# A vision block on one NeuronCore: nine token tiles of 128 in place of twelve of 96

## The reference, cut to what matters

```python
h = patches @ W.T + b                                  # 768 -> 192
# first block (input: layernorm of h)
x = _ln(x, ln1_w, ln1_b)
k, v, sr = h @ Wk_a.T, h @ Wv_a.T, sigmoid(h @ Wr_a.T)
y = bi_wkv(decay / Tn, first / Tn, k, v)               # scan over the 36 tokens, both ways, per channel
x = x + sr * y @ Wo_a.T
h = _ln(x, ln2_w, ln2_b)
x = x + sigmoid(h @ Wr_f.T) * (square(relu(h @ Wk_f.T)) @ Wv_f.T)
# second block (input: layernorm of h)
qkv -> softmax attention, 12 heads of 16, within each image -> proj
top-2 of 8 experts per token, each 192 -> 768 -> 192 with gelu
```

## Time and profile before

| | us |
|---|---|
| median of 3 runs (lowest, highest) | 360.93 (359.34, 362.2) |
| the profiled execution | 360.52 |
| its span, first to last instruction | 358.7 |
| PE busy / DVE busy / ACT busy in the span | 328.8 / 209.2 / 188.9 |

### The profile page before, as it was taken

One profiled execution on the slowest core, in us unless ns is written; L12 is line 12 of the kernel. 1 busy time (PEld: TensorE's weight loads), 2 busy tenths in 40 slices (PEclk: granted clock), 3 DMA queues, 4 the chain that ended last, 5 costly groups with the idle time before them and its releaser, 6 DMA issues.

```text
span 358.7 us, 7680 instructions
## 1 busy us (share of the span) xinstructions
PE 328.8 (92%) x2651; PEld 284.8 (79%) x2651; DVE 209.2 (58%) x580; ACT 188.9 (53%) x505; POOL 84.3 (24%) x85
## 2 busy tenths in 40 slices
...
GB/s 268 354 232 0 3 0 1 0 2 0 0 2 0 153 319 122 261 47 48 243 118 108 60 80 92 68 55 76 49 38 43 53 54 54 38 43 55 63 31 25
...
## 3 DMA queue, kind: packets, MB, share of 16 engines
...
## 4 chain that ended last, share of the span: by engine, by line
PE 44%; DVE 15%; DMA 12%; ACT 12%; issue 11%; POOL 2%; DVEq 1%; POOLq 1%; ACTq 0%
DMA out<-ffn 11%; PE banks L1318 7%; PE banks L1348 7%; PE banks L1319 6%; PE banks L1564 3%; PE banks L1415 3%; PE banks L1547 2%; PE banks L1389 2%; PE banks L1459 2%; PE banks L1390 2%; PE banks L1471 2%; ACT patch L842 1%; POOL rs L635 1%; DVE st L974 1%; ACT xh L718 1%
## 5 line engine op out<-in xcount | busy, mean ns | idle before, releaser
L635 POOL TENSOR_TENSOR rs<-va,consts 96x6 f32<-96x6 f32 (+1 forms) x16 | 17.4, 1087 | 199.5 <-DVE va L980 101.3
L1564 PE MATMUL banks<-arena,ffn 128*128 x240 | 42.9, 329 | 0.0
L667 POOL DMA_INDIRECT out<-ffn x20 | 32.3, 1617 | 44.1 <-DVE ffn L1275 37.4
L1564 PEld LDWEIGHTS banks<-arena,ffn 128*128 128x128 f32 x240 | 38.5, 190 | 0.6 <-issue 0.2
L906 ACT ACTIVATE ffn<-banks,chans 128x128 f32<-128x128 f32 x21 | 9.6, 458 | 52.9 <-PE banks L1537 52.9
L657 POOL DMA_INDIRECT vs<-xh_scratch,ffn x21 | 21.9, 1041 | 17.6 <-DVE ffn L1242 9.3
L1415 PE MATMUL banks<-rvw,ffn 128*96 128x192 f32 x144 | 25.4, 327 | 0.5 <-ACT ffn L814 0.5
L1348 PE MATMUL banks<-arena,patch 128*96 128x192 f32 x144 | 25.0, 327 | 0.0
L1348 PEld LDWEIGHTS banks<-arena,patch 128*96 128x96 f32 x144 | 23.1, 163 | 1.7 <-issue 1.2
L1415 PEld LDWEIGHTS banks<-rvw,ffn 128*96 128x96 f32 x144 | 23.3, 163 | 0.8 <-ACT ffn L814 0.8
L738 ACT ACTIVATE ht<-banks,chans 128x288 f32<-128x288 f32 (+1 forms) x24 | 12.6, 583 | 19.3 <-PE banks L1363 19.2
...
## 6 DMA issues: line engine op xcount, KB each, us to landing
...
```

What stands on the lines that cost most here:

```text
L635: pool.tensor_tensor(dst, src, const_("power", T)[:, 0:n * GTILES], ALU.pow).then_inc(rstd_ready, 1)
L667: pool.indirect_dma_start(out[:, :], bass.IndirectOffsetOnAxis(ap=IS[:, j:j + 1], axis=0), YG[j % 2], None, compute_op=ALU.add).then_inc(s ...
L1564: ins = mm(ps[:, 0:C], HST[j % 2][:, 128 * k:128 * (k + 1)], W2[:, bass.ds(e, 1), C * k:C * (k + 1)], start=(k == 0), stop=(k == HB - 1))
```

## The change

Tokens now lie in nine tiles of `T = 128`. Token stages and layer norms work on *batches* of whole tiles, two or three tiles each, listed per kind of layer norm in `BATCH`: tiles 0-2, 3-4, 5-6, 7-8 for the first norm and 0-1, 2-3, 4-5, 6-8 for the other three. The channel stages `kvr` and `qk`, the scans and the attention keep groups of eight images (288 tokens), so their borders no longer fall on those of the batches: `kvr` and `qk` wait for every batch that holds a part of their group, and the reload of values (`vl`) for every stored batch that it needs. `kf` works on batches, 256 or 384 columns. In `wo` the scan's output is laid out by groups and its result by tiles, so `cuts` splits the matmuls of a tile where a group ends. `HT` now holds all 1152 tokens for all four norms in place of `HT` and `HTB` with two groups each, and the waits of `ht_readers` are gone. `OT` holds all tokens too. `ORDER` is written anew; ScalarE takes patches from tile 5 on in place of tile 6; `kvrw` is loaded after the fourth patch tile in place of the fifth. The expert stage is the same.

```diff
-T = 96
-GTILES = GT // T
+T = 128
...
+SPLIT = (0, 2, 4, 6, TILES)
+BATCH = {"a": (0, 3, 5, 7, TILES), "2": SPLIT, "b": SPLIT, "g": SPLIT}
+BT = 3
+
+
+def tiles_of(kind, g):
+
+    return range(BATCH[kind][g], BATCH[kind][g + 1])
+
+
+def slice_of(kind, g):
+    return slice(BATCH[kind][g], BATCH[kind][g + 1])
+
+
+def batch_of(kind, t):
+    return next(g for g in range(G) if t in tiles_of(kind, g))
+
+
+def batches(kind, lo, hi):
+
+    return range(batch_of(kind, lo // T), batch_of(kind, (hi - 1) // T) + 1)
+
+
+def cuts(t, n):
+
+    marks = sorted({T * t, T * t + T} | {x for x in range(0, TOK, n) if T * t < x < T * t + T})
+    out = []
+    for lo, hi in zip(marks, marks[1:]):
+        a, b = lo - T * t, hi - T * t
+        if a == 32 and b > 64:
+            out += [(lo // n, 32, 64), (lo // n, 64, b)]
+        else:
+            out.append((lo // n, a, b))
+    return out
...
 ORDER = """
-tok:0 tok:1 tok:2 stats:a:0 apply:a:0 tok:3 tok:4 tok:5 turn:a:0 kvr:0:0 kvr:1:0 stats:a:1 apply:a:1 turn:a:1 kvr:0:1
-wkv:0:0 kvr:1:1 tok:6 sub:0:0 sub:0:1 sub:0:2 wexp:0:0 wexp:0:1 wkv:0:1 wkv:0:2 wkv:0:3 wexp:0:2 sub:0:3 wexp:0:3
-wexp:0:4 tok:7 wkv:0:4 wkv:0:5 tok:8 tok:9 tok:10 tok:11 kvr:2:0 stats:a:2 stats:a:3 apply:a:2 kvr:2:1 apply:a:3
-turn:a:2 turn:a:3 wexp:0:5 wkv:0:6 rc:0 wkv:0:7 kvr:0:2 kvr:0:3 wkv:1:0 kvr:1:2 kvr:2:2 wo:0 wo:1 kvr:1:3 wkv:1:1
-sub:1:0 sub:1:1 wexp:1:0 wexp:1:1 sub:1:2 sub:1:3 hx:0 hx:1 stats:2:0 apply:2:0 wexp:1:2 wexp:1:3 wkv:1:2 wexp:1:4
-wkv:1:3 wkv:1:4 wkv:1:5 kvr:2:3 turn:2:0 kf:0:0 kf:1:0 stats:2:1 apply:2:1 wexp:1:5 wkv:1:6 rv:0 rv:1 turn:2:1 rc:1
-wkv:1:7 rv:2 kf:0:1 kf:1:1 ff:0 stats:b:0 apply:b:0 wo:2 hx:2 wo:3 hx:3 turn:b:0 stats:2:2 stats:2:3 apply:2:2
-apply:2:3 rv:3 rv:4 qk:0 spread:0:0 rv:5 ff:1 stats:b:1 spread:1:0 turn:2:2 turn:2:3 sc:0:0 vt:0 s:0 exp:0 kf:0:2
-kf:1:2 s:1 s:2 exp:1 s:3 sc:1:0 s:4 s:5 vl:0:0 vl:1:0 vm:0:0 exp:2 exp:3 exp:4 exp:5 apply:b:1 vm:1:0 rv:6 rv:7 rv:8
-ff:2 pt:0 pt:1 turn:b:1 pv:0 pv:1 pt:2 pt:3 stats:b:2 apply:b:2 ot:0 ot:1 pv:2 pv:3 kf:0:3 ot:2 ot:3 qk:1 spread:1:1
-vt:1 vl:0:1 vl:1:1 spread:0:1 turn:b:2 proj:0 base:0 stats:g:0 kf:1:3 apply:g:0 sc:0:1 sc:1:1 s:6 s:7 s:8 s:9 vm:0:1
-vm:1:1 exp:6 exp:7 s:10 s:11 rv:9 exp:8 exp:9 exp:10 exp:11 rv:10 rv:11 ff:3 pt:4 pt:5 turn:g:0 pv:4 pv:5 qk:2
-spread:1:2 logits:0 spread:0:2 vt:2 pt:6 pt:7 stats:b:3 apply:b:3 ot:4 ot:5 pv:6 pv:7 sc:0:2 s:12 s:13 ot:6 ot:7
-turn:b:3 vl:0:2 vl:1:2 exp:12 s:14 s:15 exp:13 exp:14 vm:0:2 proj:1 stats:g:1 apply:g:1 sc:1:2 s:16 qk:3 spread:0:3
-spread:1:3 exp:15 vt:3 exp:16 s:17 exp:17 sc:0:3 s:18 s:19 s:20 s:21 turn:g:1 pt:8 pt:9 pv:8 pt:10 exp:18 exp:19
-exp:20 vm:1:2 logits:1 pv:9 pt:11 sc:1:3 s:22 vl:0:3 exp:21 s:23 ot:8 ot:9 pv:10 pv:11 vl:1:3 exp:22 exp:23 pt:12
-ot:10 ot:11 pt:13 base:1 proj:2 vm:0:3 pv:12 pv:13 vm:1:3 pt:14 pt:15 ot:12 ot:13 pv:14 pv:15 stats:g:2 apply:g:2
-ot:14 ot:15 proj:3 stats:g:3 turn:g:2 logits:2 apply:g:3 turn:g:3 base:2 base:3 logits:3
+tok:0 tok:1 tok:2 stats:a:0 apply:a:0 tok:3 tok:4 tok:5 turn:a:0 kvr:0:0 stats:a:1 apply:a:1 turn:a:1 kvr:0:1 wkv:0:0
+wkv:0:1 kvr:1:0 wkv:0:2 kvr:1:1 sub:0:0 wexp:0:0 sub:0:1 sub:0:2 wexp:0:1 sub:0:3 wexp:0:2 wexp:0:3 wexp:0:4 wkv:0:3
+kvr:2:1 tok:6 wkv:0:4 wkv:0:5 tok:7 tok:8 kvr:2:0 wexp:0:5 stats:a:2 stats:a:3 apply:a:2 apply:a:3 turn:a:2 turn:a:3
+wkv:0:6 rc:0 wkv:0:7 kvr:0:2 kvr:0:3 wkv:1:0 wkv:1:1 kvr:2:2 wo:0 hx:0 wo:1 kvr:1:3 hx:1 sub:1:0 sub:1:1 wexp:1:0
+wexp:1:1 wkv:1:2 stats:2:0 kvr:1:2 sub:1:2 wkv:1:3 wexp:1:2 sub:1:3 wexp:1:3 wexp:1:4 apply:2:0 turn:2:0 kvr:2:3
+wexp:1:5 wkv:1:4 wkv:1:5 stats:2:1 kf:0:0 apply:2:1 kf:1:0 wkv:1:6 rc:1 wkv:1:7 rv:0 rv:1 turn:2:1 wo:2 hx:2 ff:0 wo:3
+hx:3 stats:2:2 stats:2:3 apply:2:2 apply:2:3 kf:0:1 kf:1:1 turn:2:2 turn:2:3 stats:b:0 apply:b:0 turn:b:0 rv:2 rv:3
+ff:1 kf:0:2 kf:1:2 vt:0 stats:b:1 apply:b:1 turn:b:1 rv:4 qk:0 rv:5 spread:0:0 spread:1:0 kf:0:3 kf:1:3 ff:2 stats:b:2
+apply:b:2 turn:b:2 vl:0:0 vm:0:0 sc:0:0 sc:1:0 s:0 s:1 exp:0 exp:1 s:2 exp:2 s:3 s:4 s:5 exp:3 exp:4 rv:6 rv:7 exp:5
+rv:8 ff:3 vt:1 pt:0 pt:1 vl:1:0 stats:b:3 qk:1 spread:1:1 spread:0:1 vt:2 apply:b:3 turn:b:3 pv:0 pv:1 pt:2 pt:3 ot:0
+sc:0:1 s:6 sc:1:1 s:7 s:8 s:9 s:10 exp:6 exp:7 vm:1:0 qk:2 spread:1:2 s:11 spread:0:2 ot:1 pv:2 pv:3 vl:0:1 vl:1:1
+exp:8 exp:9 exp:10 exp:11 vt:3 ot:2 sc:0:2 s:12 vm:0:1 vm:1:1 s:13 s:14 exp:12 exp:13 sc:1:2 s:15 s:16 s:17 pt:4 pt:5
+qk:3 spread:0:3 ot:3 spread:1:3 pv:4 pv:5 pt:6 proj:0 stats:g:0 pt:7 ot:4 pv:6 ot:5 pv:7 vl:0:2 vl:1:2 apply:g:0
+sc:0:3 s:18 exp:14 exp:15 exp:16 exp:17 s:19 s:20 s:21 vm:0:2 pt:8 pt:9 ot:6 ot:7 pv:8 exp:18 exp:19 exp:20 pv:9
+proj:1 vm:1:2 exp:21 turn:g:0 sc:1:3 s:22 pt:10 stats:g:1 s:23 exp:22 vl:0:3 pt:11 ot:8 ot:9 exp:23 pv:10 pv:11 vl:1:3
+logits:0 vm:0:3 ot:10 pt:12 apply:g:1 pt:13 base:0 proj:2 stats:g:2 ot:11 turn:g:1 vm:1:3 pv:12 pv:13 pt:14 pt:15
+ot:12 ot:13 apply:g:2 pv:14 pv:15 turn:g:2 ot:14 ot:15 proj:3 stats:g:3 logits:1 logits:2 apply:g:3 base:1 base:2
+base:3 turn:g:3 logits:3
...
-TOK_BY_ACT = range(6, TILES)
+TOK_BY_ACT = range(5, TILES)
...
-        HTB = KVRW[:, :, :].rearrange("p b n -> p (b n)").rearrange("p (r b t) -> p r b t", r=2, b=2)
+        OT0 = KVRW[:, :, :].rearrange("p b n -> p (b n)")
...
-        XH = sb("xh", [T, 2 * GTILES, C])
-        HT = sb("ht", [128, 2, 2, GT])
+        XH = sb("xh", [T, 2 * BT, C])
+        HT = sb("ht", [128, 2, TOK])
...
-        OT = sb("ot", [128, 2, 2, GT])
+        OT1 = sb("ot1", [128, TOK])
+        OT = (OT0, OT1)
...
-        NACT = 10
+        NACT = 8
...
-                if t == 4:
+                if t == 3:
...
+                    lo = GT * g + GT // 2 * half
+                    for part in batches("b", lo, lo + GT // 2):
...
-                    for job in ht_readers(STEPS, step):
-                        full(act, job)
...
-                                turned_(pe, "a", g)
+                                for part in batches("a", GT * g, GT * (g + 1)):
+                                    turned_(pe, "a", part)
...
-                    c, half = divmod(g, 2)
-                    pe.wait_ge(z_ready, c + 1)
-                    for i, t in enumerate(group_tiles(g)):
+                    for t in tiles_of("2", g):
                         ps = begin(("wo", t))
-                        z0 = Z[c][:, GT * half + T * i:GT * half + T * (i + 1)]
-                        z1 = Z[c][:, CI * NT + T * i:CI * NT + T * (i + 1)]
-                        end(over_channels(ps[0:T, 0:C], (WOW[:, 0, :], WOWODD if half else WOW[:, 1, :]), (z0, z1)), ("wo", t))
+                        pe.wait_ge(z_ready, (T * t + T - 1) // (2 * GT) + 1)
+                        for c, lo, hi in cuts(t, 2 * GT):
+                            at = T * t - 2 * GT * c
+                            mm(ps[lo:hi, 0:C], Z[c][:, at + lo:at + hi], WOW[:, 0, :], start=True, stop=False)
+                        for n, lo, hi in cuts(t, GT):
+                            at = CI * NT + T * t - GT * n
+                            ins = mm(ps[lo:hi, 0:C], Z[n // 2][:, at + lo:at + hi], WOWODD if n % 2 else WOW[:, 1, :], start=False, stop=True)
+                        end(ins, ("wo", t))
                 elif kind == "kf":
                     need("kfw", "rfw", "vfw")
...
-                            turned_(pe, "b", g)
-                        end(over_channels(ps[:, 0:GT], h_(g, 0, GT, HTB), w_(QKVW, 128 * w, 128 * (w + 1))), (n, g))
+                            for part in batches("b", GT * g, GT * (g + 1)):
```

More of the change, by code:

```diff
@@ L147, in jobs_of @@
     kind, x = step[0], step[-1]
-    tiles = range(GTILES * x, GTILES * (x + 1))
     if kind in ("tok", "rv"):
@@ L157, in jobs_of @@
     if kind == "wo":
-        return [("wo", t) for t in tiles]
+        return [("wo", t) for t in tiles_of("2", x)]
     if kind == "kf":
@@ L163, in jobs_of @@
     if kind == "vt":
-        return [("vt", t) for t in tiles]
+        return [("vt", t) for t in tiles_of("b", x)]
     if kind == "sc":
@@ L169, in jobs_of @@
     if kind == "proj":
-        return [("proj", t) for t in tiles]
+        return [("proj", t) for t in tiles_of("g", x)]
     if kind == "logits":
```

192 lines of the change are left out of this document (93 added, 99 removed).

## The result

The changed kernel takes 348.67 us (median of 4 runs, 347.99 to 350.51), the kernel before beside it 361.07: a ratio of 0.9669 (95% interval 0.9615 to 0.9722). The prediction, 351 us in 343.5 to 358.5, held. A later comparison of the same two gave 0.9711 (0.9657 to 0.9766), 349.92 to 362.07. The profiled execution took 347.99 us, its span 345.8. PE is busy 310.9 us in place of 328.8, DVE 196.3 in place of 209.2.

What follows compares the result with a forecast made beforehand. DVE was taken to lead from 28.1 to 115.1 us, then PE to the last `proj`. Terms -1.5 -5.0 -3.2 +1.7 -1.4 = -9.4 on 360.5 us gave 351 us; range 343.5 to 356, or to 358.5 without two rivals.

Steps and rivals of the forecast that it cites:

- To the first scan, -1.5: Start to the first scan (28.1 us before): fewer tiles needed for `kvr:0:1` and `kvr:1:0` moved behind it, -1.5 us.
- First half of the scan, -5.0: To the second scan's start: three `tok` tiles instead of six, shorter norms and fewer DVE waits, -5.0 us (-3 to -6).
- Second half, -3.2: Second scan to its end: fewer `wo` and norm tiles, `rv` moved, one POOL wait gone, -3.2 us.
- From there to the last `proj`, +1.7: End of the scan to the last `proj`, led by PE's list: less work but more idleness and lower clock, +1.7 us.
- +2.0: Start of the stage behind the scan: PE idle 4 us against some 2 before, waiting on ScalarE's `kf`, +2.0 us.
- +2.2: Attention after `rv`: 44 us of PE work follow against 34 before, the added 10 us bring +2.2 us of idleness.
- +0.9: PE comes out of the scan from about 8 us of idleness, so its clock is low: +0.9 us.
- Tail, -1.4: Behind the last `proj`: `list` saves 1.2, smaller tables 1.0, `logits:1` adds 0.8; net -1.4 us.
- rival (d): All PE stages: a 128-column instruction costs 4/3, PE saves nothing, only DVE's half of the scan gains; 359 us, 5%.
- Rival (a): Whole kernel: the lists keep PE fed everywhere and all 20 us of PE's saving count; 340.5 us, 13%.
- Rival (b): Attention runs looser: PE's share falls from 79% to 70% because of ScalarE; 359 us, or 355 halfway, 12%.
- Rival (c): Attention's four groups run one after another; no gain at 18.6 us a group, 366 us at 20; slower, 5%.

Runs made afterwards that it cites:

- e4: Changed kernel with the statistics of tiles 3 and 4 ahead of the first apply and both turns ahead of `kvr:0:0`, fewer fillers: 347.86 us, ratio 0.9581 to the kernel before.
- e7: Changed kernel with only `turn:a:1` (and its batch's norm) moved ahead of `kvr:0:0`, fillers adjusted: 349.14 us, ratio 0.9626 to the kernel before.
- e6: Changed kernel with ten fillers (about 3.3 us) on PE before `turn:2:0`: 349.8 us, ratio 0.9658 to the kernel before.
- e8: Changed kernel with `kf:0:1` moved ahead of `wo:2` on PE: 352.62 us, ratio 0.9750 to the kernel before.
- e12: The changed kernel itself, measured again without an edit: 349.92 us, ratio 0.9711 to the kernel before.
- e5: Changed kernel with the loads of experts 4 to 7 issued right behind the first reload of values: 344.73 us, ratio 0.9535 to the kernel before.
- e9: Changed kernel with the second batch's six squarings of `kf` on DVE in place of ScalarE: 349.85 us, ratio 0.9631 to the kernel before.
- e11: Changed kernel with joint early statistics and turns, expert loads behind the first reload, and `kf:0:1` ahead of its batch's statistics: 343.11 us, ratio 0.9512 to the kernel before.
- e1: Changed kernel put back to tiles of 96 and the old order and fillers, keeping the new buffers: 361.67 us, ratio 0.9969 to the kernel before.
- e3: Changed kernel with the loads of experts 4 to 7 issued after the last reload of values: 353.99 us, ratio 0.9764 to the kernel before.

## Why the prediction was right, and where it was not

The prediction counted to the start of the last `proj`, the table to its end, 2.2 and 2.4 us later. Differences are to the one profile of before.

- **To the first scan, -1.5: a step that failed.** It is +1.1 in the first profile, and +0.2 to +1.2 in seven executions of this start. In the first profile 0.6 of it is a late patch, which the prediction had only in its bound. Another 0.8 lies between the end of `tok` and `kvr:0:0` (2.5 us, before 1.7): 0.5 of it is the bias of `tok:5` on PE, since ScalarE now takes patches from tile 5 on, a term that "PE does six `tok` tiles as before" left out. And moving `kvr:1:0` behind was worth 0.3 us, not 1.0 (from `kvr:0:0` to `kvr:0:1` 4.6 us, before 4.9), because `kvr:0:1` waits for ScalarE's place in the order, not for PE's four instructions. DVE's norm of two tiles was not early either: it stands behind the wait for POOL. e4 moves both and gets 1.9 us; e7 moves one and gets nothing. The prediction counted instructions on PE where the orders of ScalarE and DVE set the time.
- **First half of the scan, -5.0: -4.7.** The remaining wait for the reciprocal was put at 1.2 us and is 1.21.
- **Second half, -3.2: -3.7.** The end of the scan was forecast for 105.4 and comes at 107.9: 2.6 us late from the start, 0.3 from the first half, and 0.5 made good in this one. From the first scan to `z1` the forecast was 78.8, measured 78.7. e6 and e8 show that this stretch belongs to DVE: neither 3.3 us of fillers nor three blocks of `kf` more on PE move it by 0.1.
- **From there to the last `proj`, +1.7: -2.2 in the first profile, +0.4 in e12: the step that was furthest off.** The work was counted well: PE's busy time in this stage is 102.8 us before and 99.0 in e5, where the clock stays at 1.00, so -3.8 for -3.4. The idleness was not. It was put at +2.0 and +2.2, and PE is idle 7.6 us before, 5.9 in the first profile and 4.3 in e5: -1.8 and -3.4 in place of +4.2. The clock was put at +0.9; the rest of the first profile, PE's 102.3 busy us against e5's 99.0, is +3.3.
  - The +2.0 for the start of the stage: the gaps are there (1.10, 0.51 and in other executions 0.27 us) and their cause was named rightly (ScalarE's `kf` behind `apply:2:2` and `apply:2:3`; e9 and e11 point to the order, not the amount). But in the first 20 us behind `z1` PE is idle 1.8 us, before 2.0, where 4 were forecast, so the term came to nothing.
  - The clock: the low clock in the scan, behind PE's gaps there, cost nothing (e6). Behind `z1` it was still 1.00 and fell later, behind the gaps of 1.10 and 0.51 us, which cost 1.2 us in the first profile and in e4 and nothing in six others.
  - That all of `rv` is done at 160, and that 55 us follow, was forecast and is 161.0 and 55.0. The reasons were not right, and they cancelled. The 44 us of work at a share of some 80% turned out as 50.9 busy us at 93% (before 39.8 of 45.1 to the end of `proj`). And "the reloads of values stay hidden" is wrong: e5 shows that 3.7 us of the 55 come from the place of the expert loads. The idleness taken over from before as a rate stood for waits that could be moved.
- **Tail, -1.4: -3.5**, but in ten executions of the same code the tail is 128.3 to 135.6 us, so the size is luck. `list` took 2.84 us for 5.00, of which 0.8 is size (3.62 us for 96 instructions at full clock in e1) and 1.4 a clock that was low in the profile of before (0.68 in that window).
- **A tile of 128 costs PE what one of 96 does** (rival (d)) under 192 moving columns: 1.95 us for 12, and 11.93 us for the 72 of `tok:0` to `tok:5` both in before and in e3, e6 and e9. By the rule of the Trainium skill ("TensorE: Matmul & The Clock Gate", section "LDWEIGHTS (loading the stationary operand)") the time of a load goes with its columns. The loads do last longer here, 189 ns against 162, but under 192 moving columns that shows nowhere. Under the 8 moving columns of `logits` it does, as the prediction took it: two instructions follow two others after 0.22 us with 128 stationary columns and after 0.17 with 96, a ratio of 4/3.
- Rival (a): PE's busy time fell by 17.9 us and the time by 12.4, so not all of it counts. Rival (b): PE's share between the last `rv` and the last `proj` rose, from 88 to 93%, and did not fall. Rival (c): from the first scores (151.4) to the last `proj` (213.6) a group took 15.6 us, under the 18.6 of no gain.

The sum was right within 0.7% by luck: a start forecast 2.6 us too well stood against a stage behind the scan and a tail forecast 6.0 us too badly (3.9 and 2.1). Only the middle, -8.2 against -8.3, was right on its own, with its waits.
